# x moved to the head of the load queue, the first batch's row scaling moved from GpSimd to ScalarE, and four gate operations spread over four slots

## What is computed

```python
mod = (_silu(L0_c) @ L0_wmod).reshape(L0_c.shape[0], 6, 1, -1)
sa, ca, ga, sb, cb, gb = (mod[:, 0], mod[:, 1], mod[:, 2], mod[:, 3], mod[:, 4], mod[:, 5])
ga = (2 * (ga >= 0) - 1) * jnp.maximum(jnp.abs(ga), 0.25)
gb = (2 * (gb >= 0) - 1) * jnp.maximum(jnp.abs(gb), 0.25)
h = _layernorm(x, axis=-1) * (1 + ca) + sa
x = x + ga * _L0_attn_ref(h, ...)
h = _layernorm(x, axis=-1) * (1 + cb) + sb
x = x + gb * _L0_ffn_ref(h, ...)
# in the attention, 16 query heads, 4 key heads, width 128:
q = q * cos + _rotate_half(q) * sin
k = k * cos + _rotate_half(k) * sin
q = q / (jnp.linalg.norm(q, axis=-1, keepdims=True) + EPS) * query_scale
k = k / (jnp.linalg.norm(k, axis=-1, keepdims=True) + EPS) * key_scale
scores = jnp.tanh(scores / CAP) * CAP      # then a window mask, softmax, @ v, @ wo
```

## Time and profile before

| | us |
|---|---|
| median of 3 runs | 872.45 (872.13 to 873.22) |
| the profiled execution, its own time | 872.15 |
| its span in the trace | 870.3 |
| PE busy | 819.0 (94%) |
| DVE busy | 556.4 (64%) |
| ACT busy | 390.4 (45%) |
| POOL busy | 352.7 (41%) |

### The profile page before, as it was taken

How to read it: one execution, slowest core, us unless ns; L and a number is a source line. 1 busy time by engine, 2 the same in 40 slices (tenths; PEclk the granted TensorE clock), 3 DMA queues, 4 the chain that set the end, 5 groups by cost and what they waited for, 6 DMA issues and landing times.

```text
span 870.3 us, 14203 instructions
## 1 busy us (share of the span) xinstructions
PE 819.0 (94%) x5118; PEld 726.0 (83%) x5118; DVE 556.4 (64%) x1116; ACT 390.4 (45%) x588; POOL 352.7 (41%) x474
## 2 busy tenths in 40 slices
PE   8889999999999999999999986795999999999996
PEld 7678989989989989899899875785788888888885
DVE  4688686686686686685775734538555565555657
ACT  3565555555555555455554541523232332332321
POOL 2787587576676686675685623000000000000000
PEclk8999999999999999999999999577999999999999
DMA  8201200000000000000000000310100101100001
GB/s 318 84 26 39 78 8 1 2 2 1 1 2 1 2 1 1 2 1 2 1 2 1 2 1 8 79 37 0 37 6 32 37 1 37 36 0 0 1 25 73
DMA packets 7470, 21.42 MB, mean 25 GB/s; under 512 B 1384, under 2 KB 3560, under 8 KB 7280
## 3 DMA queue, kind: packets, MB, share of 16 engines
q1 hardware_dynamic: 6832, 20.31, 6.8%
q10 hardware_dynamic: 576, 0.28, 0.1%
HBM read 18.47 MB, written 2.11 MB: 24 GB/s over the span
## 4 chain that ended last, share of the span: by engine, by line
PE 83%; DVE 11%; issue 2%; POOL 1%; DMA 1%; ACT 1%; ACTq 0%; POOLq 0%; DVEq 0%
PE ps_o L481 13%; PE ps_proj L380 4%; PE ps_proj L382 4%; PE ps_proj L381 4%; PE ps_g L380 3%; PE ps_turn L425 3%; PE ps_g L382 3%; PE ps_g L381 3%; PE ps_u L382 3%; PE ps_u L380 3%; PE ps_u L381 3%; PE ps_d L380 3%; PE ps_d L381 3%; PE ps_d L382 3%; PE ps_y L380 3%; PE ps_y L381 3%
## 5 line engine op out<-in xcount | busy, mean ns | idle before, releaser
L481 PE MATMUL ps_o<-vaug,probs 128*128 128x129 f32 x1024 | 135.8, 275 | 8.3 <-DVE o_rows L940 6.7
L481 PEld LDWEIGHTS ps_o<-vaug,probs 128*128 128x128 f32 x1024 | 128.1, 191 | 15.6 <-issue 8.9
L734 ACT ACTIVATE ps_s<-ps_s 128x1024 f32<-128x1024 f32 x64 | 64.6, 1009 | 133.0 <-PE ps_s L382 133.0
L1205 POOL TENSOR_TENSOR root<-ssq,powers 128x4 f32<-128x4 f32 x80 | 82.7, 1034 | 83.5 <-DVE ssq L908 83.0
L936 DVE RECIPROCAL rden<-ps_o 128x2 f32<-128x2 f32 x128 | 21.7, 170 | 147.0 <-PE ps_o L481 146.9
L1108 DVE TENSOR_TENSOR mid<-ps_u,silu 128x512 f32<-128x512 f32 x64 | 44.2, 691 | 111.0 <-PE ps_u L382 110.7
L827 ACT ACTIVATE silu<-ps_g 128x512 f32<-128x512 f32 x64 | 38.2, 598 | 154.0 <-PE ps_g L382 153.9
L1216 POOL TENSOR_TENSOR prod<-prod 128x512 f32<-128x512 f32 x80 | 103.4, 1293 | 0.0
L911 DVE TENSOR_TENSOR prod<-ps_proj,cs 128x1024 f32<-128x1024 f32 x80 | 97.2, 1215 | 0.0
L1221 POOL TENSOR_TENSOR rows<-prod,rnorm 128x512 f32<-128x512 f32 x80 | 88.4, 1105 | 15.1 <-POOL prod L1216 8.6
L380 PE MATMUL ps_proj<-w_hi,h_hi 128*128 128x512 f32 x192 | 83.2, 433 | 0.8 <-DVE w_lo L891 0.8
(11 more groups left out here) (150 smaller groups left out, 2004.1 us busy)
## 6 DMA issues: line engine op xcount, KB each, us to landing
raw_e<-in_we SPq DMA_DIRECT2D x8, 768.0 KB, 4.2
raw_p<-in_wqkv SPq DMA_DIRECT2D x6, 512.0 KB, 7.5
raw_e<-in_wo SPq DMA_DIRECT2D x4, 512.0 KB, 12.2
out<-acc SPq DMA_DIRECT2D x4, 512.0 KB, 2.6
x_all<-in_x SPq DMA_DIRECT2D x1, 1792.0 KB, 7.1
x_all<-in_wmod SPq DMA_DIRECT2D x1, 1024.0 KB, 9.9
gates_a<-gate_rows_dram SPq DMA_DIRECT2D x1, 1024.0 KB, 5.6
gates_b<-gate_rows_dram SPq DMA_DIRECT2D x1, 1024.0 KB, 6.9
```

Of the source, the lines that this page charges most:

```text
L481: mm = pe.matmul(ps_o[:, h * (D + 1):(h + 1) * (D + 1)], probs[:, s % 2, at:at + P], vaug[:, b % 2, k, i // 2, :], start=(h == 0 and k == ...
L734: act.activation(ps_s[:], ps_s[:], ACT.Tanh).then_inc(tanh_done, 1)
L1205: pool.tensor_tensor(root[:, n % 2, :], ssq[:, n % 2, :], powers[:, 0:4], ALU.pow).then_inc(root_ready, 1)
```

## The change

It has three parts.

**x first.** The 256 KB of x for batch 0 are issued first in SP's queue, ahead of the modulation weights; before, ACT's queue issued them, between `cT` and `powers`.

**Row scaling.** In batch 0, Rn leaves POOL. ACT does it, in four activations of 128x128, one per head, since the scale of an activation is one value per partition. A unit that is first in its slot has its Rn behind the squares of the slot's second unit; a pending one has it behind the squares of the next slot's first unit, and so, from slot 0 on, behind that slot's tanh and exp. Batches 1 to 7 are as before. POOL keeps Sn.

**Gates.** The four operations come one each after slots 4, 5, 6 and 7.

```diff
@@ sync
+            sp.dma_start(x_all[:, 0:TT, :], a["x"][:, 0:TT, :]).then_inc(x_in[0], 16)
             sp.dma_start(wmod_sb[:, :, 0:2 * E], a["wmod"][:, :, 0:2 * E]).then_inc(wmod_in[0], 16)
@@ scalar
             act.dma_start(cT[:], a["cT"]).then_inc(c_in, 16)
-            act.dma_start(x_all[:, 0:TT, :], a["x"][:, 0:TT, :]).then_inc(x_in[0], 16)
             act.dma_start(powers[:], a["powers"]).then_inc(powers_in, 16)
...
+            def unit_rows(b, p):
+
+                if b or PROJ[p][0] == "v":
+                    return
+                n = rot_of(p)
+                act.wait_ge(rot_sum, n + 1)
+                act.wait_ge(rnorm_ready, n + 1)
+                if n >= RING:
+                    act.wait_ge(rope_turned, n + 1 - RING)
+                for h in range(4):
+                    mm = act.activation(rows[:, n % RING, h, :], prod[:, n % 2, 0, h, :], ACT.Copy, scale=rnorm[:, n % 2, h:h + 1])
+                mm.then_inc(rows_ready, 1)
...
                 for bb, p in units[:1]:
                     square(bb, p)
+                for bb, p in pending:
+                    unit_rows(bb, p)
                 for bb, r in turns[:1]:
                     turned(bb, r)
                 for bb, p in units[1:]:
                     square(bb, p)
+                for bb, p in units[:1]:
+                    unit_rows(bb, p)
                 for bb, r in turns[1:]:
                     turned(bb, r)
@@ vector
-            def gate_values():
-                dve.wait_ge(gate_rows, 1)
...
+            def gate_value(step):
+                dve.wait_ge(gate_rows, max(1, step))
+                if step == 1:
+                    dve.scalar_tensor_tensor(gabs, grow, -1.0, grow, ALU.mult, ALU.max).then_inc(gate_rows, 1)
...
-                if s == 4:
-                    gate_values()
+                if 4 <= s < 8:
+                    gate_value(s - 3)
@@ gpsimd
                 pool.tensor_tensor(whole, whole, turned, ALU.add).then_inc(rot_sum, 1)
+                if b == 0:
+                    return
```

More of the change, by code:

```diff
@@ L746, in o_head, with slot @@
                 act.activation(oT_hi[:].rearrange("p t h q -> p (t h q)"), ps_turn[:, n % 2, :], ACT.Copy).then_inc(o_hi, 1)
-            def slot(s):
+            def slot(s, pending):
                 b, i = divmod(s, SLOTS)
@@ L770, in slot @@
                     split_w(c)
+                return units[1:]
             def columns(n, src):
@@ L784, in _ @@
             split_w(1)
-            slot(FIRST)
+            pending = slot(FIRST, [])
             columns(1, ps_o[:])
@@ L789, in _ @@
             for s in range(FIRST + 1, LAST + 1):
-                slot(s)
+                pending = slot(s, pending)
             act.wait_ge(stage_a_done, 1)
@@ L967, in aggregate @@
                     dve.bn_aggr(mv2[:, TT * b + t, :], stats2[:, t, :]).then_inc(x2_aggr, 1)
-            def gate_values():
-                dve.wait_ge(gate_rows, 1)
[L971 to L976, removed]
+            def gate_value(step):
+                dve.wait_ge(gate_rows, max(1, step))
+                if step == 1:
+                    dve.scalar_tensor_tensor(gabs, grow, -1.0, grow, ALU.mult, ALU.max).then_inc(gate_rows, 1)
+                elif step == 2:
+                    dve.tensor_scalar(gsgn, grow, 0.0, 2.0, ALU.is_ge, ALU.mult).then_inc(gate_rows, 1)
+                elif step == 3:
+                    dve.tensor_scalar(gsgn, gsgn, -1.0, None, ALU.add).then_inc(gate_rows, 1)
+                else:
+                    dve.scalar_tensor_tensor(gfin, gabs, 0.25, gsgn, ALU.max, ALU.mult).then_inc(gate_rows, 1)
             def slot(s, pending):
```

## The result

The changed kernel takes 877.59 us (median of 5 runs, 876.24 to 878.40) against 872.45 (median of 5). The ratio is 1.0056, 95% interval 1.0041 to 1.0070: 5.1 us slower. The forecast was 876.3, within 872.6 to 880.0. The execution whose profile is read here took 878.40, the slowest of its five.

A forecast was written before the change was run, and what follows sets the result against it. PE fills 94% of the 870.3 us span, so only its idle or filler time can be won. Losses 0.8 + 3.6 + 1.4 less 1.6 won make 4.2 us on 872.15, so 876.3, range 872.6 to 880.0.

The forecast's parts named there:

- the clock: Rival: PE idle 3.8 us in slot 0 lowers the granted clock, 1.8 us more at most, 878.0; chance 0.20.
- slots 1 to 3: Old waits move along and new ones come for turn 9 and `h_lo`: 1.4 us lost, bounds 3.3 won, 2.9 lost.
- up to scores 0: Slots -3 to -1: ACT's later split and DVE's low part delay slot 0's scores, 0.8 us lost, start's gain included.
- slot 0: Turn 5 waits for R5 behind tanh, table load, exp and squares on ACT: 3.6 us lost, bounds 3.3 to 3.9.
- gates: Four gate operations on DVE, one a slot, remove PE's 1.60 us wait: 1.6 us won, 1.0 at the low end.
- T: Time of one row scaling on ACT, four activations in a row: taken as 1.3 us, between 1.0 and 1.6.
- dear scalings: Rival: row scalings on ACT take 1.6 us each, with new waits in slot 3: 879; chance 0.08.
- x first helps P0: At the start, x ahead in SP's queue lets P0 begin 0.6 us earlier, with ends 0 and 0.9.
- what is late next is `ident`: At the start, the transposes wait for `ident`, landing near 9.5, so they start at 9.6 to 10.1 us.
- The chain R2, second `kT_hi`, split, low part: Slot -2: ACT's weight split stands behind R2 and `kT_hi`, its low part follows on DVE, P5 starts at 31.45.
- the 6 below which the prediction called itself wrong: Test of the forecast: it is wrong if PE idle from 36 to 75 us is below 6 us.
- The rival in which the late PE catches up: Slots 1 to 3: half of 3.3 us idle used, 1.2 us lost, 873.3; chance 0.15 for catching up in part.

The follow-up runs named there:

- e1: Kernel before with only x first in SP's queue: 873.02 us, ratio 0.9999 to the kernel before.
- e6: Changed kernel with ten unused fp32 filler matmuls on PE ahead of turn 5: 876.70 us, ratio 1.0054 to the kernel before.
- e2: Kernel before with only the four gate operations spread over slots 4 to 7: 871.00 us, ratio 0.9982.
- e3: Kernel before with only the row scaling of batch 0 moved to ACT: 879.25 us, ratio 1.0081.
- e4: Changed kernel with row scaling back on POOL, so x first and gates only: 870.56 us, ratio 0.9979 to the kernel before.
- e5: Changed kernel with R5 on ACT ahead of slot 0's tanh instead of behind the squares of P6: 878.48 us, ratio 1.0066 to the kernel before.
- e7: Changed kernel with R0 to R3 on ACT and R5 to R11 back on POOL: 872.45 us, ratio 1.0009 to the kernel before.
- e8: Changed kernel with R0 to R3 back on POOL and R5 to R11 on ACT: 876.82 us, ratio 1.0045 to the kernel before.
- e9: As e5, with the high part of slot 0's weight split also ahead of R6 on ACT: 874.53 us, ratio 1.0025 to the kernel before.
- e12: Changed kernel with R5 alone back on POOL: 877.86 us, ratio 1.0055 to the kernel before.
- e10: As e2, with the powers load ahead of x in ACT's queue: 872.27 us, ratio 0.9994 to the kernel before.

## Why the prediction was right

The sign and the place held, and the sum did, in part by luck: the clock, priced at nothing in it (some 2 us), and slots 1 to 3, priced 1.1 us too high, were two errors that cancelled in part. By its own steps, with the ruler of slot starts (one execution; slots not listed make up the last 0.03):

| step | forecast | measured |
|---|---|---|
| up to scores 0 | 0.8 | 1.68 |
| slot 0 | 3.6 | 4.57 |
| slots 1 to 3 | 1.4 | 0.28 |
| gates | -1.6 | -1.83 |
| sum at slot 17 | 4.2 | 4.67 |

**One scaling.** T was taken as 1.3; the row is 1.28, and the group by form gives the mean of one activation:

```profile
L716 ACT ACTIVATE rows<-prod,rnorm 128x128 f32<-128x128 f32 x40 | 12.8, 393 | 7.0 <-POOL prod L1236 6.1 <-DVE rnorm L936 1.0
```

393 ns each, and 1.28 for four, is an overlap of about 0.1 at each of the three joints. The estimate from the Trainium skill (ScalarE: Activation LUTs, section "What ACT_TABLE_LOAD costs") was 1.27: a fixed part, a part for the pointer, a little overlap. The trace agrees. The bound of 1.6 for dear scalings is refuted.

**The start.** That x first helps P0 was wrong as a step. Its profiled execution did start P0 0.32 us earlier, but alone it wins nothing (e1). The step that failed is "what is late next is `ident`". In the changed kernel `ident` landed at 9.7, as forecast, but PE came at 10.21. In one profile, e6, it was so (1.16 us of waiting for `ident`, transposes at 9.99); in the other eight with x first PE came to the transposes late from its own queue, which begins with the modulation weights, and x is now ahead of these. PE's products on them started at 6.1 to 6.7 us with x first and at 5.2 to 6.0 without. In the executions in which they took 3.55 us, P0 stood at 14.41 and 14.46 without x first (e2, e3) and at 14.69 to 15.46 with it (e1, e4, e5, e7, e8, e9, e12). The prediction had looked at DVE's and POOL's side of the transposes and not at PE's.

**Slots -3 to -1.** The chain R2, second `kT_hi`, split, low part was right: P5 at 31.52, forecast 31.45. Scores 0 came 0.9 later than forecast, and that is the clock, by the count of the waits above and by e7: there the clock had not yet fallen, and the way from P5 to the scores took 4.92 us with 1.92 of waits, 1.2 less than in the changed kernel.

**Slot 0.** The turn waited 3.81 us, forecast about 3.8. PE was idle for 8.3 us from 36 to 75, above the 6 below which the prediction called itself wrong. The 1.0 above the term is the matmuls of P7 at half pace.

**Slots 1 to 3.** This term was mis-sized. The wait of 1.64 us ahead of the weighted sum shrank to 0.53, so 1.1 was caught up, against 0.35 lost at half pace. Turn 9 did not wait at all: PE was busy with P10 until 64.50, and R9 was done by then. The wait for `h_lo` was 0.69 for 1.0. The rival in which the late PE catches up thus held in part.

**Clock.** This was a rival of 0.20, and it came true in both places in which PE stood idle for over 2 us: in slot 0, as it said, and in slot -1, where nothing had been forecast. Its price in slot 0 is 1.0 (e6), below its bound of 1.8, and in slot -1 another 1.2. The measured 877.59 lies nearer to this rival's 878.0 than to 876.3. The forecast was near because too much loss in slots 1 to 3 stood for the missing clock, and that is luck.

**Gates.** 1.83 at their place, and 0.18% alone (e2). Nobody waited for the later write and read-back.

**What moved the time.** Two chains meet on PE within one slot: turn 5 behind R5, and the weighted sum behind R6, the split and `o_rows`. The prediction named the second only as the reason that idle time isn't regained, and in the changed kernel the second does hang on the first, by P7 and R6. e5 and e12 show that it bounds slots 0 and 1 on its own as well, and e9 that shortening both wins what shortening the first did not. The second alone was never shortened; the 0.53 us that the weighted sum waits in the changed kernel speaks for little to be won there. Open is what makes up e9's last 4.0 us against e4, 3.4 of them in the trace at slot 17: 0.6 is there at scores 0, 1.5 more at scores 1 and 0.9 between slots 3 and 4, and no run took these apart.

## What to carry to other kernels

When work is moved to another engine, its place in that engine's order can cost more than its duration: 1.28 us of scaling made PE wait 3.81, since a tanh, a table load and an exp stood ahead of it. Before moving one link, list every chain that runs through the same slot, and see what each would be with the first one gone. Removing a single wait won 0 here, because the next chain was as long. To advance a load, look at what it is put ahead of: both times a load was moved forward here, another one on the critical side became late.

## What the runs showed of the hardware

- The granted clock fell to its lower level after idle times of PE far shorter than the 9.32 us of the earlier trace rows: 2.15 us (slot -1) and 3.81 us (slot 0). The wait of 2.15 us ahead of P5 is in seven profiled executions. In six the fall came between 0.2 us before PE's return and 1.4 us after it, and the way from P5 to the scores took 4.91 to 6.09 us, the less the later the fall. In e7 it came 5 us later, after 1.92 us more of idle time. After 1.64 us in e9 it did not fall. What decides this was not measured.
- In the first 12 us the clock's record doesn't tell the pace. The six filler matmuls ahead of the transposes took 0.91 us in e6, at a granted clock of 0.87 to 1.00, and 1.63 in e2, at 1.00. Which pace a start gets was not settled.
- An 8 KB load issued ahead of the 256 KB of x made x land 2.0 us later (e10 against e2). 0.5 of it is the later issue (1.71 for 1.23); the rest is a longer way from issue to landing, and no run shows why.
